# A two-layer decoder on one core: attention scores of lane pairs in four 32-row groups, and written orders of the pieces

## What is computed

```python
x = x + L0_attn(layernorm(x))         # 16 heads of 16, 4 key heads, rotary, 50*tanh(s/50), causal
x = x + L0_xattn(layernorm(x), ctx)   # 16 heads of 64, causal mask, so only 112 context rows count
x = x + L0_ffn(layernorm(x))          # 256-1024-256, gelu, with products of tokens added to the weights
x = x + L1_attn(layernorm(x))         # 8 heads, keys and values from 2 latents of 32, causal
x = x + L1_xattn(layernorm(x), ctx, mask)   # 16 heads of 16 over 375 masked keys, context normalised
x = x + L1_ffn(layernorm(x))          # the best 2 of 4 experts; each is a whole encoder layer
```

## Time and profile before

| | us |
|---|---|
| runs | 3442.37, 3447.11, 3447.35 |
| median | 3447.11 |
| span of the profiled execution | 3440.4 |
| PE, DVE, ACT, POOL busy in it | 3307.1, 2123.6, 1940.5, 378.0 |

### The profile page before, as it was taken

The page is one execution under the profiler, slowest core; times in us unless marked ns, Lnnn a source line. Parts: engine busy times, 40 slices in busy tenths (PEclk is TensorE's granted clock), DMA queues, the critical chain, the costliest instruction groups (busy, mean ns, idle before and its releaser), DMA issues. The chain is left out here.

```text
span 3440.4 us, 79739 instructions
## 1 busy us (share of the span) xinstructions
PE 3307.1 (96%) x30487; PEld 2486.5 (72%) x30487; DVE 2123.6 (62%) x6895; ACT 1940.5 (56%) x6527; POOL 378.0 (11%) x457
## 2 busy tenths in 40 slices
PE   7999999999799999999999999997999999999998
PEld 5777777777666666666666666665888888888887
DVE  4666666666355555555545455554777767777776
ACT  2666566655444444454444545444767667767775
POOL 1112111211000000000000000000111111111111
PEclk9999999999899999999999999997999999999999
DMA  3000000000201010100000000005010022021000
GB/s 118 13 14 15 16 13 14 15 16 16 64 1 30 11 30 11 30 11 23 18 18 22 18 22 18 17 2 200 15 18 15 15 60 60 15 60 18 15 15 11
DMA packets 63957, 95.58 MB, mean 28 GB/s; under 512 B 7218, under 2 KB 59010, under 8 KB 62034
## 3 DMA queue, kind: packets, MB, share of 16 engines
q1 hardware_dynamic: 55202, 82.74, 7.9%
q0 software_dynamic: 8368, 7.70, 1.9%
HBM read 72.04 MB, written 18.37 MB: 26 GB/s over the span
## 5 line engine op out<-in xcount | busy, mean ns | idle before, releaser
L1422 DVE CUSTOM_DVE_ANT_0 PON<-pps,PMR 112x375 f32<-112x375 f32 x512 | 260.0, 545 | 265.0 <-PE pps L1168 264.4
L1656 PE MATMUL bps<-BXT,Bwexp 128*128 128x112 f32 x3072 | 373.3, 279 | 9.1 <-DMA Bwexp<-in_we 3.5
L1656 PEld LDWEIGHTS bps<-BXT,Bwexp 128*128 128x128 f32 x3072 | 362.3, 194 | 26.4 <-ACT BXT L1781 14.6
L1764 ACT ACTIVATE BPT<-bps,Blow 112x112 f32<-112x112 f32 x1024 | 349.1, 392 | 20.5 <-DVE Blow L1881 20.0
L1301 ACT ACTIVATE PPT<-pps,mcol 125x896 f32<-125x896 f32 x192 | 193.3, 1007 | 201.5 <-PE pps L1187 201.1
L1764 ACT ACTIVATION_READ_ACCUMULATOR BPT<-bps,Blow 112x1 f32 x1024 | 250.0, 246 | 0.0
L1729 PE MATMUL bps<-Bwexp,BPT 128*112 128x256 f32 x1024 | 235.4, 381 | 0.0
L892 POOL TENSOR_TENSOR rstd<-var,nhalf 112x1 f32<-112x1 f32 (+1 forms) x96 | 149.5, 1557 | 709.9 <-DVE var L810 470.1
L1168 PE MATMUL pps<-PKT,PQM 64*112 64x375 f32 x1024 | 222.2, 513 | 3.7 <-DVE Pmx L1422 1.7
L708 ACT ACTIVATE PT<-PT,low 112x112 f32<-112x112 f32 x512 | 191.8, 386 | 37.6 <-DVE low L867 37.6
L1456 POOL TENSOR_TENSOR Prstd<-Pvar,nhalf 112x1 f32<-112x1 f32 x128 | 72.0, 565 | 1281.2 <-DVE Pvar L1336 1281.2
(11 more groups left out here) (308 smaller groups left out, 7297.9 us busy)
## 6 DMA issues: line engine op xcount, KB each, us to landing
Bwexp<-in_we SPq DMA_DIRECT2D x7, 2311.0 KB, 22.5
PCX<-in_ctx SPq DMA_DIRECT2D x24, 375.0 KB
out<-BY POOLq DMA_DIRECT2D x64, 112.0 KB, 3.0
BXIN<-xmid SPq DMA_DIRECT2D x61, 112.0 KB, 2.0
Bwexp<-in_we SPq DMA_DIRECT2D x7, 770.0 KB, 5.1
Brexp<-in_re SPq DMA_DIRECT2D x7, 672.0 KB, 9.5
XIN<-in_x SPq DMA_DIRECT2D x32, 112.0 KB
CX<-in_ctx SPq DMA_DIRECT2D x32, 112.0 KB
```

Of the source, the lines that this page charges most:

```text
L1422: m = v.tensor_tensor_reduce(out=ON[s][0:T, i * LC:(i + 1) * LC], in0=bank[s][i][0:T, 0:LC], in1=MR[s][:, :], scale=1.0, scalar=-3.0e38, o ...
L1656: m = mm(o[:, j * T:(j + 1) * T], wt[:, c, n0 + j * 128:n0 + (j + 1) * 128], rhs[:, c, :], start=(c == 0), stop=(c == 1))
L1764: m = A(PT[s][0:T, h, :], bank[s][i][0:T, v * T:(v + 1) * T], ACT.Exp, scale=0.25, bias=low[s][:, h:h + 1], accum_out=sums[s][:, h:h + 1])
```

## The change

Scores are computed in 32-row groups. The masked copies become two (`QM[128, 2, 2, T]`, mask `hm2`, the sum of two halves of `hm4`, made by one new DVE operation at the start). In a group of 32 rows lie two heads, of which each copy keeps one, and the array holds four such groups at a time: two for each lane of a *pair*, (0, 1) or (2, 3), each with its own bank. The even lane's piece waits for both lanes' semaphores (through `tallies`) and issues both lanes' matmuls; the odd lane's piece of the same place is empty. `half` makes the odd lane take the groups in the other order, so that the four matmuls that stand together use four different groups. The other pieces (maxima, tanh, exponentials, products) stay per lane and read other indices.

Sizes: L583's two matmuls of 448 columns become four of 224 for each lane, L1187's likewise; L1130 becomes two pieces of 4 matmuls a lane, the second waiting for the first's own end; there the queries and the latent keys are stored unmasked (`QL`, `KL`), and the two ACT copies of L1276 become one. `msel` shrinks from [128, 8, 125] to [128, 4, 125], `lscale` goes, the DVE operations L829, L1413 and L1872 go from 128x448 to 128x224.

`run_slots` and its tables go. Each engine of each pass has a string, `ORDER[...]`, in which a digit is the lane whose next piece is issued; "4" is a piece of the preparation (`fold`, `keep`) in pass 1. DMAs are the same, their order among lanes is new. In pass 1 `OS` moves to the second half of the query tile; in pass 3 DVE's wait for the output's DMA is loosened by 16 for each lane number.

The core of the diff: `half`, a score piece of each kind, the order.

```diff
+        rows = [slice(32 * j, 32 * j + 32) for j in range(4)]
...
+        def half(s, step):
+
+            return step if s % 2 == 0 else 1 - step
...
-                        if r == 0:
-                            t.wait(la_ready[s])
-                        else:
-                            t.wait(mx_ready[s])
-                        for i in range(2):
-                            m = mm(bank[s][i][0:T, 0:LC], QM[s][side[i], r // 4, r % 4, :], KT[s][side[i], r // 4, :], start=True, stop=True)
-                        m.then_inc(s_psum[s], 1)
+                        if s % 2 == 0:
+                            for k in (s, s + 1):
+                                tallies[k].wait(mx_ready[k] if r else la_ready[k])
+                            step, (c, v) = r // 4, divmod(r % 4, 2)
+                            for k in (s, s + 1):
+                                for i in range(2):
+                                    g = rows[2 * half(k, step) + i]
+                                    m = mm(bank[k][i][0:T, 0:LC], QM[k][g, c, v, :], KT[k][g, c, :], start=True, stop=True)
+                                m.then_inc(s_psum[k], 1)
...
-                    for c in range(C2):
-                        for k in range(KT3):
+                    for step in range(2):
+                        for kt in range(KT3):
                             yield
-                            if k:
-                                t.wait(p_ready[s])
-                            elif c:
-                                t.wait(sp_ready[s])
-                            else:
-                                t.wait(small_ready[s])
-                            for v in range(4):
-                                for i in range(2):
-                                    mm(bank[s][i][0:KP, v * T:(v + 1) * T], msel[side[i], 4 * c + v, :], MXT[s][side[i], :],
-                                       start=(v == 0), stop=False, skip_group_check=True)
-                            for i in range(2):
-                                m = mm(bank[s][i][0:KP, 0:QW], KT[s][side[i], c, k * KP:(k + 1) * KP], QM[s][side[i], c, :, :],
-                                       start=False, stop=True, skip_group_check=True)
-                            m.then_inc(st_psum[s], 1)
+                            if s % 2 == 0:
+                                for k in (s, s + 1):
+                                    tallies[k].wait(p_ready[k] if kt else sp_ready[k] if step else small_ready[k])
+                                for n in range(4):
+                                    for k in (s, s + 1):
+                                        for i in range(2):
+                                            g = rows[2 * half(k, step) + i]
+                                            mm(bank[k][i][0:KP, n * T:(n + 1) * T], msel[g, n, :], MXT[k][g, :],
+                                               start=(n == 0), stop=False, skip_group_check=True)
+                                for c in range(C2):
+                                    for k in (s, s + 1):
+                                        for i in range(2):
+                                            g = rows[2 * half(k, step) + i]
+                                            m = mm(bank[k][i][0:KP, c * 2 * T:(c + 1) * 2 * T], KT[k][g, c, kt * KP:(kt + 1) * KP], QM[k][g, c, :, :],
+                                                   start=False, stop=True, skip_group_check=True)
+                                        if c == C2 - 1:
+                                            m.then_inc(st_psum[k], 1)
...
-                        for v in range(4):
-                            for i in range(2):
-                                m = mm(bank[s][i][0:T, v * T:(v + 1) * T], QM[s][side[i], c, v, :], KT[s][side[i], c, :], start=True, stop=True)
-                        m.then_inc(s_psum[s], 1)
...
+                            for n in range(4):
+                                for k in (s, s + 1):
+                                    for i in range(2):
+                                        g = rows[2 * half(k, step) + i]
+                                        m = mm(bank[k][i][0:T, n * T:(n + 1) * T], QM[k][g, n // 2, n % 2, :], KT[k][g, n // 2, :], start=True, stop=True)
+                                    if n == 3:
+                                        m.then_inc(s_psum[k], 1)
...
-                run_slots(pe, LANES, quarter, batch, TURNS["pe2"], TURNS["lead2"], FIRST["pe2"], LAST["pe2"])
+                run_order(pe, ORDER["pe2"], batch, quarter)
```

More of the change, by code:

```diff
@@ L262, in skip, with run_order @@
         self.seen[sem.num] = self.seen.get(sem.num, 0) + n
-class Place:
-    def __init__(self, n, last=False):
-        self.n, self.last, self.first = n, last, False
-def run_slots(eng, lanes, count, batch, turns, lead, first, last, aside=None):
-    at, runs = Place([0] * len(lanes)), [None] * len(lanes)
-    before = [sum(1 for x in turns[s] if x < lead[s]) for s in lanes]
-    def begin(s):
-        runs[s] = [batch(s, at), 0]
-    def work(s, places, turn, end):
-        while runs[s][1] < end and places[runs[s][1]] <= turn:
-            next(runs[s][0], None)
-            runs[s][1] += 1
-    def middle(i):
-        at.n = [i] * len(lanes)
-        for turn in range(SPAN):
-            for s in lanes:
-                local = (turn + lead[s]) % SPAN
-                if local == 0:
-                    at.n = [i + 1 if k == s and lead[s] else at.n[k] for k in lanes]
-                    begin(s)
-                work(s, turns[s], local, len(turns[s]))
-    for s in lanes:
-        if lead[s]:
-            begin(s)
-    at.first = True
-    others = aside(at) if aside else iter(())
-    for turn in range(SPAN):
-        for s in lanes:
-            if lead[s]:
-                work(s, first[s], turn, before[s])
-        if turn >= 400 and turn % 20 == 0:
-            next(others, None)
-    for _ in others:
-        pass
-    at.first = False
-    for i in range(count - 1):
-        middle(i)
-    at.n, at.last = [count - 1] * len(lanes), True
-    for s in lanes:
-        if not lead[s]:
-            begin(s)
-    for turn in range(SPAN):
-        for s in lanes:
-            work(s, last[s], turn, len(turns[s]))
+def run_order(eng, order, batch, count, extra=None):
+    runs = {4: extra} if extra else {}
+    begun = {s: 0 for s in LANES}
+    for mark in order:
+        s = int(mark)
+        if s == 4:
+            next(runs[4], None)
+            continue
+        if s not in runs:
+            runs[s], begun[s] = batch(s, begun[s]), begun[s] + 1
+        if next(runs[s], "over") == "over":
+            runs.pop(s)
+    assert all(n == count for n in begun.values()) and set(runs) <= {4}
+    for _ in runs.get(4, ()):
+        raise AssertionError("pieces left over")
 def span_of(sems):
@@ L506, in fold @@
                         yield
-                    for _ in range(5):
-                        yield
                     pe.wait_ge(all_prepared, 2)
@@ L517, in fold @@
                             yield
-                    for _ in range(12):
-                        yield
                     pe.wait_ge(all_prepared, 3)
@@ L961, in build @@
             yo = W("yo", C2)
-            rows = [slice(32 * j, 32 * j + 32) for j in range(4)]
             first_loaded, row_loaded = cast_ready, bias_ready
```

416 lines of the change are left out of this document (262 added, 154 removed), and 180 rows, old and new, of tables (FIRST, LAST, TURNS).

## The result

The changed kernel takes **3498.29 us** (median of 4 runs, 3494.64 to 3503.45), the kernel before beside it 3446.17: a ratio of 1.0157 with a 95% interval of 1.0143 to 1.0171. It is slower by 1.6%, inside the predicted range and on the other side of no change than the forecast of 3435. The profiled execution took 3503.45 us, its span 3501.8, against 3440.4 before.

What follows compares the result with a forecast made beforehand. PE was taken as the bound in all three passes. Changes of +2 (pass 2), +20 (pass 1) and -34 us (pass 3) sum to -12, added to the median 3447.1: 3435 us, range 3280 to 3520.

Steps and rivals of the forecast that it cites:

- 322 us off PE's work: All passes: one score piece feeding two lanes halves its PE time, saving 229 us in pass 2, 30 in pass 1, 63 in pass 3.
- rival 3: Score pieces: four row groups don't run four at a time; 3656 us, or 3501 at three quarters of the speed; chance 0.10.
- for the beginnings and ends of passes I take 0 (-5 to +10): Start and end of each pass: no change in time, 0 us, with bounds -5 to +10.
- parts at nothing: Smaller copies, merged ACT copy, selection table, DMA orders, table loads and the moved weight-folding marks: priced at no time.
- 178.0 against 177.7: Pass 2's round: forecast length against the length before, in us; the pass gives back all that it saves.
- A: Pass 2's round, eight score pieces of lanes 0,1: DVE needs 28.8 us against 17.2 of PE work.
- B: Pass 2's round, score pieces of lanes 2,3 alternating with transposed steps of lanes 0,1: 28.2 us against 18.9 on PE.
- C: Pass 2's round, transposed steps of lanes 2,3 among item ends and next starts: 25.1 us against 19.7 on PE.
- -2.1 x 16 = -34: Pass 3: 60.3 us of work plus 2.7 of waits make a 63.0 us round, 2.1 shorter, over 16 rounds.
- I add 1.6: Pass 2's round: 1.6 us for PE's clock at 0.50 after about 5 us of idling in a row.
- Rival 2: Pass 2's score stretches: idling holds PE's clock at half; 3480 us for one stretch, 3557 for both; chance 0.10.
- such waits come to 6.3: Pass 1's round: PE waits, as behind tanh, exponential and mask, total 6.3 us; round 108.6, +20 over 8 rounds.

## Why the prediction was right and wrong

**What held.** The forecast took 322 us off PE's work, and the trace has 317 less: 246 in pass 2 (229 forecast), 61 in pass 3 (63), but 10 in pass 1 (30), so the sum fits better than its terms. Four row groups work at once, and rival 3 falls: a pair's row piece takes 0.83 us, its transposed step 1.19, which is 1.01 and 1.09 times one lane's piece before. The Trainium skill, page TensorE: Matmul & The Clock Gate, section Part 3: Packing small matmuls, states a measured speedup of 3.07 for four row tiles, from which the prediction had an estimate of 1.3 times. The trace is well below that. The waits in pass 2 stand where they were forecast, ahead of the row pieces for DVE's maxima and ahead of the transposed steps for ACT's exponentials. Taking 196 ns off each maximum brought 53 us in this kernel and 6 in the one before: shown, not only argued.

**What failed: "for the beginnings and ends of passes I take 0 (-5 to +10)".** They cost 13, 28 and 16 us, 56 together, which is most of the loss of 61. The rounds came to +5 where I had -12. No row and no walk through the new orders stood behind that 0. That the longer ends come with the orders is shown: the new pieces in the old orders have the old ends, and each lane alone in the new orders has the long ones (64, 52 and 57). What fills them differs from pass to pass.

In pass 1 PE stands idle for 8.1 us until the load of `wy` has landed, ahead of the first piece of `fold`, the preparation:

```profile
30.27 1.06 PE L364 MATMUL ps<-XT,KX 128*128 128x32 f32 x4 [8.12 <-DMA wy<-in_wa]
```

The new string has this piece in PE's fourth place, the old order as a string in the sixteenth. All six traces with the new order of pass 1 have this wait (8.1 to 8.5 us), and the eight with the old order don't. The prediction had this, too, among its parts at nothing: "The marks that fold weights move to the start, into waits for loads".

In pass 3 the new order begins with the first pieces of all four lanes, and PE waits 10.1 us for their loads, where it waited 3.8. Seven traces have the new order of this pass and wait 9.2 to 10.1 us, the other seven wait 3.7 to 3.8. The first 70 us of the pass, changed kernel and kernel before:

```profile
L1539 PE MATMUL bps<-const,BXIN 112*128 112x112 f32 x8 | 2.5, 422 | 10.1 <-DMA BXIN<-xmid 10.1
```

```profile
L1650 PE MATMUL bps<-const,BXIN 112*128 112x112 f32 x10 | 2.7, 361 | 3.8 <-DMA BXIN<-xmid 3.8
```

In pass 2 both pairs come to their row pieces nearly together. In the first round of the string the row pieces of the two pairs alternate from the sixth of lanes 0 and 1 on, with nothing else between them, where a steady round has projections of the other pair. A hundred microseconds around it, first of the changed kernel and then of the kernel before:

```profile
1025.00:1125.00 100.00, 74.42 (x784) 50.99 (x781) 59.65 (x255) 36.86 (x110) 2.84 (x5) 0.81 0.02 6
```

```profile
980.00:1080.00 100.00, 96.95 (x940) 61.36 (x938) 55.98 (x221) 48.36 (x115) 7.77 (x12) 1.00 0.05 16
```

PE works 74 of 100 us, at a mean clock of 0.81, where it worked 97 at 1.00; 9.1 us of its idle time stand ahead of row pieces, for DVE's maxima. At the end of this pass only lanes 2 and 3 are left, and PE works 18.1 of the last 27.5 us. How much of the 56 us each of these things is worth is argued from the traces; no run changed one of them alone.

**Pass 2, "178.0 against 177.7".** That the pass came out at -0.4 for a forecast of +2 is luck: its rounds gained 28 us and its ends lost 28. The round's sum has a slip as well. It takes PE's work as 177.7 - 28.6 = 149.1, but 177.7 is the round's length, of which PE is busy for 173.8; with that the sum is 174.1, and 174.2 was measured. Its terms did not come so close. From the first row piece of a pair to that of the other (A) the trace has 31.3 us for 28.8, from there to the end of the first pair's last output piece (B) 29.4 for 28.2, and the steps and output pieces of the other pair (C) take 29.6 for 25.1. More of the remaining work ran inside these stretches than I had counted. PE is busy for 150.7 of the round's 174.1 us, 87% in place of 82.

**Pass 3, "-2.1 x 16 = -34".** The undisturbed round is 63.8 us, 0.8 above the forecast 63.0. But I multiplied one steady round by 16. Four of the changed kernel's rounds take 69.8, 71.5, 72.5 and 71.1 us (in the last three the chain of waits names a load of an expert's biases and norm weights, `Brexp`); before, three rounds took 70.9, 68.9 and 66.7. They eat the gain, and the mean round does not move (66.0 to 66.1).

**The clock, "I add 1.6".** It costs 8 to 9 us in a round of pass 2 (15.2 and 18.2 us of busy time at 0.50 in two rounds). Over the pass it costs 81 us more than before, over all passes 113. In the round this was made up for: PE's work fell by 31 us where I had 28.6, and the idle time was 23 where my stretches have 27. Rival 2 was right on the place (A and B have stretches at half clock after idle ones) and wrong on the size in steady rounds, as PE is at half for 10 to 14 of the 31 us of stretch A, and not throughout.

**Pass 1, "such waits come to 6.3".** The round is 4.0 us longer (110.1; 108.6, or +2.5, was forecast), but not for the reason given. The wait ahead of the first probability product is there, 12.2 us over the pass, and without it the round stays at 109.9. Rather, the scores' busy time falls as forecast (64.5 to 34.5 us over the pass), while PE's busy time in the round hardly does (106.1 to 105.7). The old orders, with each lane's own pieces, take 106.8, and the new orders with each lane alone 109.7; so the new order holds this round. Which of its steps does stays open.

## What to carry to other kernels

When PE's work is halved by running two lanes' pieces together, count what the pair's *readers* need between two such pieces: here 2.1 us of maxima and 2.0 of exponentials stand against 0.8 to 1.2 us of matmul, and shorter readers turned part of the saving into time. A new order also changes what stands at the beginning and the end of a staged loop: loads that have not landed yet, lanes that all start together. So walk through those stretches piece by piece and price them from their own windows, and a loop's disturbed rounds from theirs, before multiplying a steady round. And weigh an order and a cheaper piece apart: each in the other's old surroundings, one kernel each, told more here than the sum of the two.

## What the runs showed of the hardware that was not expected

- Pieces of neighbouring lanes need not be issued as one to share the array. Two lanes' row pieces that stand behind each other on different row groups, each with its own wait, start all four first matmuls within 0.03 us (1600.17 in the run with each lane alone), and such sharing was worth 262 of the 276 us.
- The time at half clock does not follow the idle time. Pass 2 has 212 us of idle time and 175 us of busy time at 0.50 in the changed kernel, but 123 and 488 with two groups at a time, in a kernel whose PE is busy 92% of its span. No run shows why.
- Added work can be nearly free: 115 us more of matmuls, put where PE had waited, lengthened the span by 15.
